# Edge-type products of a relational graph layer, with stationary and moving operands exchanged

## The reference

```
def _rel_layer(h, src, dst, etype, norm, V, comp, loop_w, bias, activation):
    c = comp[etype]                      # comp: 200 x 8, etype: one per edge
    m = jnp.zeros((src.shape[0], out_dim), h.dtype)
    for b in range(num_bases):
        xb = h @ V[b]
        m = m + c[:, b, None] * xb[src]
    m = m * norm
    agg = jax.ops.segment_sum(m, dst, num_segments=h.shape[0])
    out = agg + bias + h @ loop_w
    return jax.nn.relu(out) if activation else out
...
h = _rel_layer(feats, src, dst, etype, norm, V1, comp1, loop1, bias1, True)
h = _rel_layer(h, src, dst, etype, norm, V2, comp2, loop2, bias2, False)
```

## Time and profile before

| | us |
|---|---|
| median of 3 runs | 2073.78 (2073.11 to 2077.47) |
| span of the profiled execution | 2533.6 |
| PE, DVE, ACT, POOL busy in it | 1943.2, 1535.0, 357.2, 1411.4 |
| mean granted TensorE clock in it | 0.792 |

### The profile page before, as it was taken

How to read it: one execution, slowest core, us unless ns; L and a number is a source line. 1 busy time by engine, 2 the same in 40 slices (tenths; PEclk the granted TensorE clock), 3 DMA queues, 4 the chain that set the end, 5 groups by cost and what they waited for, 6 DMA issues and landing times. The chain is left out here.

```text
span 2533.6 us, 40547 instructions
## 1 busy us (share of the span) xinstructions
PE 1943.2 (77%) x12305; PEld 1396.7 (55%) x12306; DVE 1535.0 (61%) x2202; ACT 357.2 (14%) x869; POOL 1411.4 (56%) x1527
## 2 busy tenths in 40 slices
PE   1577777778777777777748887878878788776898
PEld 1466665556556555655525555555555465554665
DVE  7887778777777777777654445555455455441243
ACT  2111221211121121122200000000000000000110
POOL 5765566656566566656266566566565566566000
PEclk7577777877777777787768788888898789886899
DMA  5232223223223222322221121112232222223354
GB/s 130 58 83 65 66 63 81 68 65 79 66 63 77 65 67 64 80 67 61 58 53 50 47 50 49 48 50 80 66 87 62 53 78 64 76 63 88 108 212 138
DMA packets 194040, 186.56 MB, mean 74 GB/s; under 512 B 109133, under 2 KB 166974, under 8 KB 193947
## 3 DMA queue, kind: packets, MB, share of 16 engines
q0 software_dynamic: 45760, 93.81, 14.9%
q1 hardware_dynamic: 140134, 87.49, 12.1%
q10 hardware_dynamic: 8052, 4.04, 0.6%
HBM read 159.75 MB, written 25.47 MB: 73 GB/s over the span
## 5 line engine op out<-in xcount | busy, mean ns | idle before, releaser
L811 POOL DMA_INDIRECT ring<-h_rows,rel_idx x1312 | 1259.7, 960 | 750.5 <-issue 377.7
L982 DVE TENSOR_TENSOR rel_pick<-rel_src_row,dve_bank 128x1664 bf16<-128x1664 int32 (+1 forms) x268 | 486.4, 1815 | 368.4 <-remote 170.8
L1269 PE MATMUL rel_ps_z<-rel_C,ring 128*128 128x56 f32 x3100 | 484.6, 307 | 134.0 <-issue 123.5
L1269 PEld LDWEIGHTS rel_ps_z<-rel_C,ring 128*128 128x128 f32 x3100 | 477.7, 229 | 171.9 <-issue 163.1
L1213 PE MATMUL rel_ps_p<-rel_h_parts,rel_pick 128*128 128x384 bf16 x1150 | 300.8, 390 | 47.6 <-issue 47.5
L1367 ACT ACTIVATE rel_ZT<-rel_ps_z 128x304 f32 x292 | 114.2, 426 | 1401.6 <-remote 688.4
L1200 PE MATMUL carried<-rel_h_parts,rel_pick 128*128 128x384 bf16 x1100 | 236.9, 367 | 61.9 <-issue 50.8
L1200 PE MATMUL rel_ps_p<-rel_h_parts,rel_pick 128*128 128x384 bf16 x1100 | 227.0, 366 | 60.3 <-issue 25.7
L1357 ACT ACTIVATE rel_A<-rel_ps_a 128x500 f32 x292 | 165.5, 602 | 533.1 <-remote 315.9
L1200 PEld LDWEIGHTS carried<-rel_h_parts,rel_pick 128*128 128x128 bf16 x1100 | 113.1, 106 | 176.1 <-issue 112.9
L1200 PEld LDWEIGHTS rel_ps_p<-rel_h_parts,rel_pick 128*128 128x128 bf16 x1100 | 117.5, 110 | 160.4 <-issue 96.7
(11 more groups left out here) (229 smaller groups left out, 1937.3 us busy)
## 6 DMA issues: line engine op xcount, KB each, us to landing
ring<-h_rows,rel_idx POOLq DMA_INDIRECT x1312
A_slabs<-rel_A SPq DMA_DIRECT2D x25, 800.0 KB
A_slot<-A_slabs SPq DMA_DIRECT2D x25, 800.0 KB, 4.4
early_slot<-A_slabs SPq DMA_DIRECT2D x18, 896.0 KB
rel_types<-edge_types SPq DMA_DIRECT2D x97, 100.0 KB
rel_src_row<-in_src_dram SPq DMA_DIRECT2D x134, 64.0 KB
last_slot<-A_slabs SPq DMA_DIRECT2D x4, 512.0 KB, 5.9
ring<-h_rows,idx_table POOLq DMA_INDIRECT x118
```

The source lines that it names most:

```text
L811: g_.indirect_dma_start(ring[:, s * CHUNK + i, :], None, rows_in, bass.IndirectOffsetOnAxis(ap=idx[which][:, n:n + 1], axis=0)).then_inc(l ...
L982: v.tensor_tensor(pick[:, b0:b0 + n, :], src_row[s][:, :].unsqueeze(1).to_broadcast(shape), node_ids[:, b0:b0 + n].unsqueeze(2).to_broadca ...
L1269: ins = m_.matmul(bank(ps_z[s], NB)[:, :, bass.ds(at[i], TW)], ring[:, first + i, :], C[s][:, i, :, :], start=False, stop=(i == n - 1))
```

## The change

The type product of layer one is turned round, in a new class `TurnedProducts` in place of `Coefficients`. The table is now the stationary operand (48 columns) and the one-hots move, 512 edges at a time: `multiply_half` makes [48, 512] in the bank with two matmuls, ACT copies it to SBUF as bf16 (`keep_half`), the second half follows through the same bank, and `fold` multiplies each tile's 128 columns of the copy by a matrix `fold` (three stacked unit matrices, 48 x 16), which turns back and adds the three parts: eight matmuls of 16 columns, [128 edges, 8 x 16]. `scale` is left with the two multiplications by the weight, reading PSUM. The parts are bf16 values picked by a one-hot, so the copy loses nothing.

```
+    def multiply_half(self, pe, m, s, half):
+        if half == 0:
+            after(pe, self.coef_ready, m)
+            pe.wait_ge(self.onehot_ready, m + 1)
+        else:
+            pe.wait_ge(self.half_kept, 2 * m + 1)
+        for h in range(2):
+            ins = self.nc.tensor.matmul(self.ps[0:self.ROWS, :], flat(self.t.comp[:, h, :, :]), self.onehot[:, s, h, half * 512:(half + 1) * 512],
+                                        start=(h == 0), stop=(h == 1))
+        ins.then_inc(self.half_done, 1)
+    def keep_half(self, act, m, half):
+        act.wait_ge(self.half_done, 2 * m + (half + 1))
+        self.nc.scalar.activation(self.turned[:, half * 512:(half + 1) * 512], self.ps[0:self.ROWS, :], ACT.Copy).then_inc(self.half_kept, 1)
+    def fold(self, pe, m):
+        pe.wait_ge(self.half_kept, 2 * m + 2)
+        for e in range(ET):
+            ins = self.nc.tensor.matmul(self.ps[:, e * 2 * NB:(e + 1) * 2 * NB], self.turned[:, e * P:(e + 1) * P], self.t.fold[:, :],
+                                        start=True, stop=True)
+        ins.then_inc(self.folded, 1)
+    def scale(self, eng, m, slot):
+        eng.wait_ge(self.folded, m + 1)
...
+            ins = self.nc.vector.tensor_tensor(into, self.ps[:, 0:ET * 2 * NB].rearrange("p (e l b) -> p l e b", l=2, b=NB)[:, l, :, :],
...
-                    hold(pool, co.product_done, at + (AHEAD + 1) if ...
+                    hold(pool, co.half_done, 2 * (at + (AHEAD + 1)) if ...
...
-            hold(pool, co.product_done, begun.get((c, h), 0))
+            hold(pool, co.half_done, 2 * begun.get((c, h), 0))
...
                         weigh(c, s, parity * CPG + j)
+                        if not (isinstance(c, int) and c + AHEAD - 1 >= ET_CHUNKS):
+                            co.scale(dve, c + (AHEAD - 1), (parity * CPG + j + AHEAD - 1) % COEF_RING)
                         build_keys(c, s)
...
-                    if layer == 0 and not (isinstance(c, int) and c + AHEAD - 1 >= ET_CHUNKS):
-                        co.scale(dve, c + (AHEAD - 1), (parity * CPG + j + AHEAD - 1) % COEF_RING)
...
                 for m in range(AHEAD):
-                    co.multiply(pe, m, m % 2)
+                    for half in range(2):
+                        co.multiply_half(pe, m, m % 2, half)
+                    co.fold(pe, m)
...
+                    if makes(g, j):
+                        co.multiply_half(pe, c + AHEAD, j % 2, 0)
                     if layer == 0:
                         sum_slab(c, j % 2, at)
...
                     if makes(g, j):
-                        co.multiply(pe, c + AHEAD, j % 2)
+                        co.multiply_half(pe, c + AHEAD, j % 2, 1)
...
+                        if makes(g, j) and i == HALF:
+                            co.fold(pe, c + AHEAD)
...
+                    if makes(g, j):
+                        co.keep_half(act, c + AHEAD, 0)
                     if layer == 0:
                         spread_slab(g, j, parity, at[2:4], 0)
                         spread_slab(g, j, parity, at[4:6], 1)
+                    if makes(g, j):
+                        co.keep_half(act, c + AHEAD, 1)
```

42 lines of the change are left out of this document (40 added, 2 removed).

## The result

The changed kernel takes 2201.57 us (median of 4 runs, 2199.64 to 2203.04), the kernel before beside it 2074.43 (4 runs, 2073.11 to 2077.47). The ratio is **1.0605, 95% interval 1.0587 to 1.0622: 127 us slower**. The forecast was 2083, with 2048 to 2125 as its range: the sign was right, the size far outside.

A forecast was written before the change was run, and what follows sets the result against it. The prediction took POOL's gathers to bound the kernel, at or within about 2% of the pace. To the median 2073.8 it added 9 us for the serial start and 0 for PE's work: 2083 us, range 2048 to 2125.

The forecast's parts named there:

- The scale moves ahead of M: DVE's order in layer one: M waits for the fold; PE loses 0 to 20 us, hidden under POOL's pace.
- POOL is the pace, or within about 2% of it: Whole kernel: POOL's 1430 gathers at 1.25 us plus its gaps sum to 2073 us, the median.
- The 460 us between profile and median: Profile of 2533.6 us against median 2073.8: the excess was taken as stalls of the profiled execution and added to nothing.
- PE's wider products: PE's type products in layer one: 62 to 123 us more work, expected to fit under POOL, barely.
- The rule on weight loads: Skill rule for PE's loads, 107 ns per 128 columns: would save about 70 us; the prediction held that the trace disagrees.
- DVE: DVE in layer one loses the sum of the parts: -64 us, 869 to 805, no gain if DVE isn't the pace.
- ACT's copies: Two PSUM copies a chunk on ACT, 119 us in all; ACT has room, counted as nothing.
- The serial start: Start of layer one: one-bank products delay the first M by 11.4 us, and POOL's long run by 9 us.
- PE becomes the pace: Rival, chance 0.17: layer one's clock under 0.81 lets PE's work exceed POOL's, giving 2112 to 2162 us.
- DVE was the pace: Rival, chance 0.22: DVE, not POOL, ruled layer one, so its relief gives 2046 to 2063 us, typically 2053.
- The start is absorbed: Rival, chance 0.14: POOL's wait before chunk 8 is slack and the loss is caught up, 2070 to 2078 us.
- Wider streams lift the clock: Rival, chance 0.05: PE's added columns raise layer one's clock from 0.74 to 0.85, giving 2040 us if PE was the pace.

The follow-up runs named there:

- b2_before: The kernel before, unchanged, traced on a chip of the sort of the recorded times: 2072.72 us (one run), span 2071.1.
- e2_third: The changed kernel with the kept row moved ahead of the scale and M in even chunks: 2088.86 us, 1.0057 of before; 1.0413 and 1.0392 on slower chips.
- e6: The kernel before with the kept row moved ahead of M in chunks with j = 0 and 2: 2047.15 us, 0.9854 of before.
- e0_before: The kernel before, unchanged, on a chip of the slower sort: 2522.24 us, 1.0001.
- b1_before: The kernel before, unchanged, traced on another chip of the slower sort: 2487.75 us (one run).
- e5: The kernel before with three more 512-column matmuls in each type product, output unchanged: 2118.96 us, 1.0201 of before.
- e4: The changed kernel with both halves and the fold later on PE, the scale at DVE's chunk end: 2062.92 us, 0.9936 of before; 1.0351 on the slower sort.
- e7: The changed kernel with halves and fold later, scale at DVE's chunk end, and the kept row ahead of M: 2049.81 us, 0.9869 of before.
- e3_order_alone: The kernel before, old products, only the scale moved ahead of M: 2555.78 us, 1.0113 of before on the slower sort; 2082.02, 1.0029 on the recorded sort.
- the first set: The first group of follow-up runs, the kernel before and three reordered kernels, on a slower chip where the kernel before took 2519.74 us.

## Why the prediction was wrong

**The step that failed** is "*The scale moves ahead of M.*" with its result "0 to 20 us, under POOL's pace hidden". It followed M to PE's next use of M, the slab, and there it was right: the slab's matmuls behind M (L1230) waited 0.6 us in the whole stretch. It did not follow the other instruction that stands behind M in DVE's queue, the kept row, which z's last tile needs *earlier* than the slab needs M. "PE has in the meantime four z tiles" is the wrong sentence: in every second chunk the fourth of those tiles waits for the kept row itself. The earlier trace rows had the order in them: M at 949.22, the kept row (L988) behind it at 955.22. In that trace DVE waits 4.39 us between the two, for a reason that the profile calls remote, and I read this as room of DVE; in b2_before the kept row follows M without a wait (854.45, 855.97) and it is PE that waits for it. Measured: moving the kept row ahead of the wait, the scale and M gives back 113 of 125 us (the change against e2_third).

**"POOL is the pace, or within about 2% of it"** was half right, and that its sum met the median was chance. The pitch of 1.25 us holds in every trace, and layer two goes by it, 1036 to 1040 us in all kernels of this sort of chip. But in layer one POOL was held 19 us, and 2047 us in e6 shows the floor to lie at least 29 below the median. The sum that met 2073 took two terms from the slower chip's trace. One is the end after the last gather, 179 us there and 154 in b2_before (1916.95 to 2071.1). The other is the change of layers, counted as a fixed 46 us, 36 in b2_before. The two are 35 us too large and stood in for what POOL really lost. The second is not even fixed: POOL runs up to four chunks ahead, and what it waits there is what PE and DVE are behind. The rows of POOL's first gather of layer two, in b2_before, the change and e6:

```profile
1032.72 0.94 POOL L834 DMA_INDIRECT ring<-h_rows,idx_table  x1 [36.34 <-POOLq L661]
```

```profile
1159.20 0.94 POOL L905 DMA_INDIRECT ring<-h_rows,idx_table  x1 [42.52 <-POOLq L732]
```

```profile
1005.59 0.94 POOL L834 DMA_INDIRECT ring<-h_rows,idx_table  x1 [21.06 <-POOLq L661]
```

36.3, 42.5 and 21.1 us. A sum of one engine's work and *all* its unheld gaps that meets the median proves the pace only if the gaps can't shrink.

**The 460 us between profile and median** were laid to the profiled execution. By e0_before and b1_before, whose spans of 2519.5 and 2486.0 meet their own timed runs, they were the chip's. The consequence was that this trace shows another picture of z's waits (3.9 us for the kept row and 123.5 by "issue", against 143.3 and 3.1 in b2_before), without the very row that would have shown the ring.

**PE's wider products**: the mechanism was right, the term too small. A pair of 512-column matmuls takes 0.55 us at the fast clock up to the next work (0.42 were taken), the eight of the fold 0.28 (0.20). Rows of the changed kernel:

```profile
888.99 0.61 PE L545 MATMUL rel_ps<-rel_onehot,comp_parts 100*48 100x512 bf16 x2
889.54 0.39 PE L1191 MATMUL rel_ps_a<-zero 128*128 128x500 bf16 x1
...
894.32 0.35 PE L557 MATMUL rel_ps<-fold,rel_turned 48*128 48x16 bf16 x8
894.60 0.88 PE L1346 MATMUL rel_ps_z<-rel_C,ring 128*128 128x56 f32 x6
```

2 x 0.55 + 0.28 = 1.38 in place of 0.41: +0.97 a chunk, 95 us in all at the fast clock, where 62 were counted. The clock of the stretch went from 0.89 to 0.85, above the 0.81 that the prediction asked for, and PE was still not the pace by its work: 170 of 1018 us are idle. That it should "fit" was the wrong question; what counts is the part of it inside the ring.

**The rule on weight loads** that was set against the trace does not give the price of a pair here: the exchange saves no PE time, with 151.1 + 35.0 us busy in its two groups against 60.7 for L482 in b2_before. A single load of L482 is on record there with a median of 96 ns, near the rule's figure, but the loads overlap each other and the matmuls, 25 ns apart in the earlier trace rows. The Trainium skill (TensorE: Matmul & The Clock Gate, "Back-to-back issue gap") gives 131 ns for a matmul of 512 columns in a sustained stream. The rows above show 0.55 us for two up to the next work, and e5 0.76 for three, about twice that for each; no run here has a longer stream of them, so the page's case itself is not tested.

**DVE** lost 49 us over the whole kernel (1530.5 to 1481.5), 64 with the gaps were forecast for layer one; the reduce that went took 53.9 in b2_before. As forecast, this gained nothing in the change, where DVE's legs of the ring grew. The reason given, that POOL is the pace, does not hold: in e4's order, with the same DVE work gone, the kernel is 13 us faster than before.

**ACT's copies** took 0.586 us (0.605 taken), and PE hardly waits for them: 8.6 us in the whole trace, 4.1 ahead of L545 and 4.5 ahead of L557, and nothing in the steady stretch. Counted nothing, right.

**The serial start** was right in its working. Each product takes 4.29 us (62.24 to 66.53; 4.6 forecast), and the first M comes at 83.95 against 72.86 in b2_before, +11.1 (+11.4 forecast). Rows of the changed kernel, first DVE, then POOL:

```profile
62.24 0.36 DVE L565 TENSOR_TENSOR coef<-rel_ps,norm_table 128x64 f32<-128x64 f32 x2 [2.60 <-PE rel_ps L557]
...
66.53 0.36 DVE L565 TENSOR_TENSOR coef<-rel_ps,norm_table 128x64 f32<-128x64 f32 x2 [2.48 <-PE rel_ps L557]
...
83.95 1.60 DVE L1020 TENSOR_TENSOR rel_M<-dve_bank,key_table 128x1400 bf16<-128x1400 f32 x1
...
123.64 0.19 POOL L855 COPY rel_idx<-idx_table 128x16 int32 x1 [7.15 <-PE rel_ps_z L1351]
```

The slab of chunk 4 starts 10.8 us later. POOL loses less: its first index copy comes at 123.64, in b2_before at 118.75 with no wait ahead of it, where the earlier trace rows had 6.13 us. What the start costs in the end is open, since no run took it away by itself. That e2_third is 12 us above before does not measure it, for e2_third has the kept row early and before has it late. The best bound is e7 against e6: its stretch begins 6.5 us later (122.0 against 115.5), and its median is 3 us higher.

**The rivals.** "PE becomes the pace" had the time nearest to the measured one (2112 to 2162), but for a reason that e4 refutes: more PE work and faster than before. "DVE was the pace" fell for the change (less DVE work brought nothing there), though its doubt of POOL was sound, and DVE, busy 92% of the steady stretch of b2_before, is the fuller engine of the ring. "The start is absorbed" fell for the change: chunk 4 starts 10.8 us late, and POOL is held more behind it, not less. "Wider streams lift the clock" fell for it too, since the clock of the stretch went from 0.89 to 0.85; in e4_again, with the same streams and 82 of 879 us idle, it is 0.92. The change streams 1408 columns more a chunk (2176 against 768), not 2048.

## What to carry to other kernels

When a wait is moved ahead of other work in an in-order queue, list every instruction behind it up to the next wait, and for each the first reader on another engine; the one that is needed soonest sets the price, not the one that was moved past. Look for rings (A waits for B's piece, B later for A's) and add up their legs: such a ring is a pace of its own, with no engine full (PE busy 79% of the stretch of b2_before, DVE 92%, both at work in it), and work added to any leg is paid, at least in part. The Trainium skill (Perfetto Trace Analysis, "Identifying the Most-Contended Engine") advises to optimise the engine of highest occupancy first, and to judge TensorE by its FLOPs and its weight loads, not by the busy time of its matmuls. With the loads as the measure it is DVE here, with 74% of b2_before against 59% for PE's loads. It is the right engine, but its occupancy does not say what helps: the gain of 29 us came from moving one 0.55 us instruction of DVE ahead of M, with no engine's work changed, and taking 49 us of work off DVE came with a loss of 125 us in one order and a gain of 13 in another.

## What the hardware showed unexpectedly

**Two sorts of chips.** The same kernel has medians of 2076 to 2077 us on three chips used here and of 2499 and 2520 on two others, 20 to 21% apart. On the slower ones engines stand still at places where nothing that the profile names is missing. The row of z on b1_before (span 2486.0), against that of b2_before above:

```profile
L1269 PE MATMUL rel_ps_z<-rel_C,ring 128*128 128x56 f32 x3100 | 469.6, 302 | 161.9 <-issue 98.6
L1269 PEld LDWEIGHTS rel_ps_z<-rel_C,ring 128*128 128x128 f32 x3100 | 463.3, 223 | 212.8 <-issue 204.4
```

"issue" takes 98.6 us ahead of these matmuls, 3.1 in b2_before. Some stalls are long: in e3_order_alone, on the first set's chip, DVE stood 16.04 us in front of the fifth product's parts, which PE had made at 73.67 in 0.82 us (PE, then DVE):

```profile
73.67 0.82 PE L482 MATMUL rel_ps<-comp_parts,rel_onehot 100*128 100x48 bf16 x16 [5.65 <-issue]
```

```profile
90.98 0.56 DVE L488 TENSOR_REDUCE rel_summed<-rel_ps 128x128 f32<-128x384 f32 x1 [16.04 <-remote]
```

What makes these chips slower, and why the repaired kernels e2 and e4 still lose 3.5 to 4% on them, is open; no run could tell. The lesson that is shown: compare a trace's span with the timed runs, and where they differ by more than a per cent, take a trace on the chip of the times before reading its waits.
